# Shifted-window block on one core: another order for the first tile and the tail, 32-column tiles for two small products

## The reference, cut to what matters

```python
xn = _ln2d(x, norm1_g, norm1_b)
xn = jnp.roll(xn, shift=(-SHIFT, -SHIFT), axis=(2, 3))
windows = _window_partition(xn, win)
attn_out = _mha(windows, in_w, in_b, out_w, out_b)   # softmax(q k^T / sqrt(8)) v, 8 heads
attn_out = attn_out @ proj_w.T + proj_b
y = shortcut + roll_back(window_reverse(attn_out))
z = _ln2d(y, norm2_g, norm2_b)
z = einsum('bchw,oc->bohw', z, fc1_w) + fc1_b
z = gelu(z)
z = einsum('bchw,oc->bohw', z, fc2_w) + fc2_b
return y + z
```

## Time and profile before

| | |
|---|---|
| median of 3 runs | 104.44 us (103.73 to 104.53) |
| the profiled execution | 104.1 us, of which 102.3 us are the span from first to last instruction |
| mean granted TensorE clock | 0.977 of full speed |
| busy: PE, PEld | 88.7 us (87%), 55.4 us |
| busy: DVE, ACT, POOL | 64.0, 46.9, 39.6 us |
| the chain that ended last | PE 51%, DVE 12%, POOL 12%, issue 11%, ACT 7%, DMA 4% |

### The profile page before, as it was taken

The page is one execution under the profiler, slowest core; times in us unless marked ns, Lnnn a source line. Parts: engine busy times, 40 slices in busy tenths (PEclk is TensorE's granted clock), DMA queues, the critical chain, the costliest instruction groups (busy, mean ns, idle before and its releaser), DMA issues.

```text
span 102.3 us, 4188 instructions
## 1 busy us (share of the span) xinstructions
PE 88.7 (87%) x1786; PEld 55.4 (54%) x1786; DVE 64.0 (63%) x168; ACT 46.9 (46%) x77; POOL 39.6 (39%) x52
## 2 busy tenths in 40 slices
PE   5999986539999989999999999989899699998550
PEld 5888862224666657668657656667566433323100
DVE  5466699768576978966976979799255713120120
ACT  0511935240954647539537442345434773834400
POOL 7069891796970742940340613407030303000000
PEclk9999999995999999999999999999999999999997
DMA  2898010111111110111110110000000000211202
GB/s 46 211 435 343 13 44 26 51 51 48 39 51 45 39 57 26 44 39 35 57 39 31 39 45 22 3 6 3 6 0 6 0 0 6 103 43 59 103 0 103
DMA packets 3523, 5.93 MB, mean 58 GB/s; under 512 B 1136, under 2 KB 1520, under 8 KB 3376
## 3 DMA queue, kind: packets, MB, share of 16 engines
q1 hardware_dynamic: 2784, 3.28, 9.4%
q10 hardware_dynamic: 720, 2.38, 6.3%
HBM read 2.64 MB, written 1.05 MB: 36 GB/s over the span
## 4 chain that ended last, share of the span: by engine, by line
PE 51%; DVE 12%; POOL 12%; issue 11%; ACT 7%; DMA 4%; DVEq 0%; POOLq 0%
PE ps_s L266 10%; PE ps_t L318 8%; PE ps_t L399 7%; PE ps_u L335 5%; POOL rstd L797 4%; PE ps_m L388 4%; ACT probs L711 4%; DMA x_tok<-x_tok_d 4%; PE ps_t L266 3%; PE ps_o L349 3%; PE ps_m L375 2%; POOL xhat L804 2%; DVE row_max L526 2%; ACT hidden L739 2%; DVE sums L540 2%
## 5 line engine op out<-in xcount | busy, mean ns | idle before, releaser
L711 ACT ACTIVATE probs<-ps_t 128x1024 f32<-128x1024 f32 x16 | 16.4, 1025 | 22.1 <-PE ps_t L318 22.1
L526 DVE TENSOR_REDUCE row_max<-ps_s 128x16 f32<-128x1024 f32 x16 | 19.4, 1215 | 6.1 <-PE ps_s L266 6.1
L266 PE MATMUL ps_s<-masked,qk 32*64 32x256 f32 x256 | 18.4, 402 | 1.6 <-ACT probs L711 0.9
L821 POOL TENSOR_TENSOR rstd<-y_var,minus_half 128x4 f32<-128x4 f32 x8 | 8.1, 1008 | 27.9 <-DVE y_var L569 27.8
L266 PE MATMUL ps_t<-masked,qk 32*64 32x256 f32 x256 | 18.4, 403 | 0.3 <-ACT probs L711 0.3
L318 PE MATMUL ps_t<-max_x,minus_sel 128*128 128x512 f32 x32 | 12.2, 463 | 0.2 <-POOL max_x L812 0.2
L266 PEld LDWEIGHTS ps_s<-masked,qk 32*64 32x64 f32 x256 | 8.8, 136 | 4.7 <-issue 2.8
L335 PE MATMUL ps_u<-probs,vz 128*32 128x64 f32 x512 | 10.5, 222 | 0.0
L812 POOL TENSOR_TENSOR max_x<-max_t,early 128x512 fp32r<-128x512 f32 x8 | 8.4, 1051 | 3.8 <-DVE max_t L534 3.8
L335 PEld LDWEIGHTS ps_u<-probs,vz 128*32 128x32 f32 x512 | 7.9, 109 | 3.6 <-issue 3.2
L232 PE MATMUL ps_t<-zeros 128*128 128x128 f32 x52 | 8.9, 329 | 1.0 <-DVE zeros L639 1.0
(11 more groups left out here) (80 smaller groups left out, 134.8 us busy)
## 6 DMA issues: line engine op xcount, KB each, us to landing
masked<-qk SPq DMA_DIRECT2D x60, 32.0 KB, 1.8
x_ch<-x_ch_d ACTq DMA_DIRECT2D x1, 1024.0 KB, 8.1
out_d<-result SPq DMA_DIRECT2D x4, 256.0 KB, 2.5
x_tok<-x_tok_d ACTq DMA_DIRECT2D x1, 512.0 KB, 6.1
late<-late_d ACTq DMA_DIRECT2D x1, 352.0 KB, 5.3
x_tok<-x_tok_d SPq DMA_DIRECT2D x2, 128.0 KB, 4.2
x_tok<-x_tok_d ACTq DMA_DIRECT2D x1, 256.0 KB, 4.9
early<-early_d ACTq DMA_DIRECT2D x1, 182.0 KB, 4.2
```

What stands on the lines that cost most here:

```text
L266: return nc.tensor.matmul(ps[L * u:L * u + L, g, n * TOK:(n + 1) * TOK], qk[r:r + RG, b, w, t], masked[r:r + RG, b, :, w, t], start=(n == ...
L526: nc.vector.tensor_reduce(row_max[:, 16 * w:16 * w + 16], ps_s[:].rearrange("q g (h j) -> q (g h) j", j=L), axis=AX.X, op=ALU.max).then_in ...
L711: nc.scalar.activation(probs[:, w, :], ps_t[:].rearrange("q g c -> q (g c)"), ACT.Exp).then_inc(probs_done, 1)
L821: nc.gpsimd.tensor_tensor(rstd2[:].rearrange("q n w -> q (n w)"), y_var[:].rearrange("q n w -> q (n w)"), minus_half[:], op=ALU.pow).then_ ...
```

## The change

- **First tile.** The identity matrix is loaded by a DMA of its own. `project_qkv(0)` is split: `project_qk(0)` first, `project_v(0)` after the scores of the tile. ScalarE copies q and k image by image, and the masks for k are made image by image (VectorE three of four heads, ScalarE one). Tile 1's transpose and projection use `ps_u` and `ps_o` (`proj_bank`), the scores of tile 0's image 1 use `ps_t` (`score_bank`). `late_products` and `late_weights` move behind them. A `first_slot` replaces slot 0 on PE, ScalarE has its own order for it. Fewer products of zeros are made.
- **Zeroing.** Four of the five `vz` buffers are zeroed by ScalarE (before its first copy) instead of GpSimd, the masked buffer 3 by VectorE at the start, buffer 2 by GpSimd at the start.
- **Tiles of the array.** `project_out` and `y_spread` use four column tiles of 32 where they used two of 64: 8 matmuls each instead of 4.
- **Tail.** `fc1(0, 0)` moves into slot 7; `fc1(0, 1)` and `fc1(1, 0)` stand ahead of `y_spread(6)` and `project_out(7)`; `y_sum(7)` moves behind `fc2(0)` and `fc1(1, 1)`; `fc2(1)` ahead of `y_spread(7)`.

```diff
         early = sb("early", [P, EARLY])
+        ident_sb = sb("ident_sb", [P, P])
+        ident = ident_sb[:]
         late = sb("late", [P, LATE])
-        ident = early[:, 0:P]
...
+        ps_uo = bank("ps_uo", 2)
+        ps_u, ps_o = ps_uo[:, 0:1, :], ps_uo[:, 1:2, :]
...
+        def proj_bank(k):
+            return ps_uo if k == 1 else ps_m
+
+        def score_bank(k, w):
+            return ps_t if k == 0 and w == 1 else ps_s
...
-            def project_qkv(k):
+            def project_qk(k):
                 pe.wait_ge(xn_copied, k + 1)
...
-                        nc.tensor.matmul(ps_m[C * s:C * s + C, w, 0:TOK], w_qkv[r, C * s:C * s + C], xn[r, k % 2, :],
-                                         start=True, stop=True, tile_position=(C * w, C * s))
+                        ins = nc.tensor.matmul(proj_bank(k)[C * s:C * s + C, w, 0:TOK], w_qkv[r, C * s:C * s + C],
+                                               xn[r, k % 2, :], start=True, stop=True, tile_position=(C * w, C * s))
+                ins.then_inc(qk_projected, 1)
+
+            def project_v(k):
+                if k == 0:
+                    pe.wait_ge(qk_copied, 1)
                 for n in range(BLK):
...
+                ins.then_inc(v_projected, 1)
+
+            def project_qkv(k):
+                project_qk(k)
+                project_v(k)
...
-                if w == 0 and k == 0:
-                    pe.wait_ge(k_masked_first, 2)
+                if k == 0:
+                    pe.wait_ge(k_masked_dve, w + 1)
+                    pe.wait_ge(k_masked_act, w + 1)
...
-                if k + w >= 1:
+                if k >= 1:
                     pe.wait_ge(max_found, 2 * k + w)
...
+                if k + w == 0:
+                    pe.wait_ge(max_found, 2)
...
+                    pe.wait_ge(w_fc1_made, 1)
...
                 for u in range(2):
-                    for w in range(2):
-                        ins = nc.tensor.matmul(o4[C * w:C * w + C, :, u, :], w_out[:, u, :], attn[:, w * P:(w + 1) * P],
-                                               start=True, stop=True, tile_position=(0, C * w))
+                    for j in range(4):
+                        w, c = j // 2, 32 * (j % 2)
+                        ins = nc.tensor.matmul(o4[32 * j:32 * j + 32, :, u, :], w_out[:, u, c:c + 32],
+                                               attn[:, w * P:(w + 1) * P], start=True, stop=True, tile_position=(0, 32 * j))
...
-                    for w in range(2):
-                        ins = nc.tensor.matmul(spread_bank(k)[C * w:C * w + C, n * P:(n + 1) * P],
-                                               rstd2[:, n, w:w + 1].to_broadcast([P, C]), ident,
-                                               start=True, stop=True, tile_position=(0, C * w))
+                    for j in range(4):
+                        ins = nc.tensor.matmul(spread_bank(k)[32 * j:32 * j + 32, n * P:(n + 1) * P],
+                                               rstd2[:, n, j // 2:j // 2 + 1].to_broadcast([P, 32]), ident,
+                                               start=True, stop=True, tile_position=(0, 32 * j))
...
-                pe.wait_ge(z_done, 2 * s + 2)
+                pe.wait_ge(z_done, TILES - 2 if s == 0 and m == 1 else 2 * s + 2)
...
                 pe.wait_ge(late_loaded, 16)
+                pe.wait_ge(v_copied, 2)
...
+            def first_slot():
+                scores_t(0, 0)
+                x_transpose(2)
+                shift_scores(0, 0)
+                late_products()
+                project_qkv(2)
+                scores_both(1, 0, 0, 1)
+                shift_scores(0, 1)
+                x_transpose(3)
+                weigh_values(0, 0)
+                scores(1, 1)
+                fc1_mean()
+                bias_of_v()
+                project_qkv(3)
+                x_transpose(4)
...
                 else:
+                    fc1(0, 0)
                     scores_t(t, 1)
...
-                if t == 0:
-                    fc1_mean()
-                    bias_of_v()
...
-            warm_up(4)
...
+            warm_up(4)
             x_transpose(0)
-            warm_up(2)
+            warm_up(1)
...
-            project_qkv(0)
-            pe.wait_ge(b_qk_made, 1)
-            late_products()
+            project_qk(0)
             warm_up(4)
             x_transpose(1)
-            warm_up(2)
+            scores(0, 0)
             project_qkv(1)
-            scores(0, 0)
-            x_transpose(2)
             scores(0, 1)
-            project_qkv(2)
-            x_transpose(3)
-            for t in range(TILES):
+            project_v(0)
+            first_slot()
+            for t in range(1, TILES):
                 slot(t)
             weigh_values(TILES - 1, 1)
             y_sum(TILES - 2)
-            fc1(0, 0)
+            fc1(0, 1)
...
+            fc1(1, 0)
             y_spread(TILES - 2)
...
             project_out(TILES - 1)
-            fc1(0, 1)
-            fc1(1, 0)
-            y_sum(TILES - 1)
             fc2(0)
             fc1(1, 1)
+            y_sum(TILES - 1)
             fc1(2, 0)
+            fc2(1)
             y_spread(TILES - 1)
-            fc2(1)
             fc1(2, 1)
             fc1(3, 0)
...
+            def mask_k_first(w):
+                if w == 0:
+                    dve.wait_ge(qk_first_copied, 1)
+                else:
+                    dve.wait_ge(qk_copied, 1)
+                for h in range(3):
+                    ins = nc.vector.tensor_scalar(masked[0:C, 0, h, w], qk[C:P, 0, w], slot_mask[C:P, h:h + 1], None,
+                                                  op0=ALU.mult)
+                ins.then_inc(k_masked_dve, 1)
...
-                dve.wait_ge(vz_zeroed, VB)
+                dve.wait_ge(vz_zeroed, 1)
+                dve.wait_ge(vz_zeroed_act, VB - 1)
...
+            for b in (0, 3):
+                nc.vector.memset(masked[:, b].rearrange("q h w t -> q (h w t)"), 0.0).then_inc(masked_zeroed[b], 1)
...
-            mask_k_first()
-            late_weights()
+            mask_k_first(0)
+            mask_k_first(1)
             find_max(0, 0)
             ln1_stats(3)
             find_max(0, 1)
             transpose_max(0)
-            nc.vector.memset(masked[:, 3].rearrange("q h w t -> q (h w t)"), 0.0).then_inc(masked_zeroed[3], 1)
+            late_weights()
...
+            def copy_qk_first():
+                act.wait_ge(qk_projected, 1)
+                act.wait_ge(b_qk_made, 1)
+                for w in range(2):
+                    nc.scalar.activation(qk[:, 0, w], ps_m[:, w, 0:TOK], ACT.Identity,
+                                         bias=b_qk[:, 0:1]).then_inc(qk_copied if w else qk_first_copied, 1)
+
             def copy_v(k):
+                if k == 0:
+                    act.wait_ge(v_projected, 2)
                 if k < VB:
-                    act.wait_ge(vz_zeroed, k + 1)
+                    act.wait_ge(vz_zeroed, 1)
+                    act.wait_ge(vz_zeroed_act, VB - 1)
...
-                for h in range(2, SLOTS):
-                    ins = nc.scalar.activation(masked[0:C, 0, h], qk[C:P, 0], ACT.Copy, scale=slot_mask[C:P, h:h + 1])
-                ins.then_inc(k_masked_first, 1)
+                for w in range(2):
+                    nc.scalar.activation(masked[0:C, 0, 3, w], qk[C:P, 0, w], ACT.Copy,
+                                         scale=slot_mask[C:P, 3:4]).then_inc(k_masked_act, 1)
...
             act.dma_start(early[:], early_d).then_inc(early_loaded, 16)
+            act.dma_start(ident_sb[:], ident_d).then_inc(ident_loaded, 16)
...
+            act.wait_ge(zeros_set, 1)
+            for b in range(1, VB):
+                nc.scalar.activation(vz[:, b].rearrange("q w n h e -> q (w n h e)"), zeros[:, 0:1].to_broadcast([P, 1024]),
+                                     ACT.Copy).then_inc(vz_zeroed_act, 1)
             copy_xn(0)
-            copy_qk(0)
+            copy_qk_first()
             mask_k_first()
-            copy_v(0)
             copy_xn(1)
             copy_qk(1)
             copy_v(1)
+            copy_v(0)
             copy_xn(2)
+            exponentiate(0, 0)
             copy_qk(2)
             copy_v(2)
+            exponentiate(0, 1)
             copy_xn(3)
-            for t in range(TILES):
+            copy_qk(3)
+            copy_v(3)
+            copy_xn(4)
+            for t in range(1, TILES):
...
             nc.gpsimd.memset(minus_half[:], -0.5).then_inc(half_set, 1)
             zero_masked(1)
+            zero_masked(2)
+            zero_values(0)
             pool.wait_ge(half_set, 1)
-            ln1_rstd(0)
-            ln1_scale(0)
-            zero_values(0)
-            ln1_rstd(1)
-            ln1_scale(1)
-            ln1_rstd(2)
-            ln1_scale(2)
-            zero_values(1)
-            zero_masked(2)
-            ln1_rstd(3)
-            ln1_scale(3)
+            for k in range(4):
+                ln1_rstd(k)
+                ln1_scale(k)
```

(2 more changed lines are left out.)

82 lines of the change are left out of this document (42 added, 40 removed).

## The result

The changed kernel took 112.96 us in the median (111.64 to 113.87) beside 104.34 us before: 1.0756 times as long, with a 95% interval of 1.07 to 1.0813. The forecast was 107.7 us, with a range that ended at 109.6. The sign was right and the size was not: the kernel is slower by over twice the forecast amount.

The account below looks back on a forecast made before the run. It took the first tile as bound by circular waits among engines, slots 3 and 4 by a PE-VectorE-GpSimd loop, the tail by project_out(7). Terms -0.5, -0.3 and +4.3 made +3.5, giving 107.7 us, range 105.6 to 109.6.

Parts of the forecast that it names:

- the lowered clock: Tail: rival that the new holes lower TensorE's granted clock, adding 1.4 us for 109.1 us; chance 12%.
- Opening, zeroings at 1.05 each: Opening: four ScalarE zeroings of 1.05 us ahead of the first xn copy put it at 9.7, about 0.85 us late.
- VectorE's second zeroing: Opening: VectorE's second zeroing, 1.76 us, ends near 5.0, making the moments 0.3 us late, covered by ScalarE.
- Early scores, first shift: First tile: scores at 12.4 against 14.95, tile 0's max_x at 17.9, first shift at 19.0, over 5 us early.
- Slot 1 starts at 29.9: End of the first tile: slot 1 at 29.9 against 30.40, a gain of 0.5 us.
- the first tile wins more: First tile: rival with ScalarE's zeroings near their low bound and VectorE on time at 22.9; 1.0 to 2.5 us more, chance 18%.
- shorter than the one that did it: Tail: new holes of 1.5, 2.1 and 1.5 us are shorter than the 2.88 us hole that lowered the clock.
- 32-column tiles, -0.3: project_out and y_spread: 0.11 us saved per slot on a mode switch, counted in slots 2, 5 and 6; gain 0.3 us.
- Slot 7, +0.8 and 0.3 given back: Slot 7: fc1(0, 0), about 1.0 us, goes into a 0.26 us hole; loss 0.8 us, of which 0.5 is left.
- Tail order, +4.3 with slot 7: Tail: project_out(7), gelu(0, 1) and fc2(0) come later, last result at 102.9 against 98.60; +4.3 us, slot 7's 0.5 included.
- faster after all: First tile: rival that all PE idle time and lowered clock there go, slot 1 before about 25; 102.5 us, chance 5%.

Follow-up runs that it names:

- e14: Changed kernel with PE's old tail order and the old, larger counts of zero products in the opening: 105.95 us, ratio 1.018.
- e15: Changed kernel with PE's old tail order and 5 + 1 products of zeros in the first tile's two holes: 104.31 us, ratio 1.0003.
- e5: Changed kernel with PE's old tail order, the opening's old zero-product counts and 5 + 1 products of zeros in the first tile's holes: 104.21 us, ratio 0.9931.
- e10: Kernel before with the new tail and products of zeros in its holes, but fc1(1, 0) back behind project_out(7): 107.09 us, ratio 1.0292.
- e12: e7 with another tail order on PE, ScalarE and VectorE, two gelus moved ahead on ScalarE: 100.35 us, ratio 0.9642 to the kernel before.
- e18: e12 with project_out and y_spread on two column tiles of 64 again: 100.56 us, ratio 0.9658.
- e11: Kernel before with only fc1(0, 0) moved into slot 7: 106.38 us, ratio 1.0113.
- e3: Changed kernel with 6, 8 and 4 products of zeros in the tail's three holes: 111.18 us, ratio 1.061.
- e9: Kernel before with the new tail and products of zeros in two holes, but y_sum(7) back ahead of fc2(0): 106.79 us, ratio 1.026.
- e7: e5 with the projection of tile 3 moved ahead of scores(1, 1): 102.25 us, ratio 0.9809 to the kernel before.
- e1: Changed kernel with PE's tail order as before and fc1(0, 0) out of slot 7: 106.87 us beside 104.02.
- e2: Kernel before with the new tail order and fc1(0, 0) in slot 7 alone: 109.75 us, ratio 1.0548.
- e13: Changed kernel, new tail included, with all products of zeros of e3, e4 and e5: 108.39 us, ratio 1.04.
- e16: e5 with project_out and y_spread on two column tiles of 64 again: 104.15 us, ratio 0.9936.
- e4: Changed kernel with 5 + 1 products of zeros in the first tile's two holes: 110.51 us, ratio 1.0611.

## Why the prediction was right and wrong, step by step

The step that failed is the walk of PE's new order at 2.4 GHz durations, with the lowered clock put aside as a rival of 12% in the tail alone. The runs show half clock in two stretches in its place, worth 2.43 us in the first tile and 1.65 in the tail.

- **Opening, zeroings at 1.05 each: nearly.** They took 0.97 (3.88 for four), `xn` came at 9.18 instead of 9.7. PE's transpose, for which the copy also waits, ends at 8.94, so the zeroings hold `xn` up by 0.24 and not by the 0.85 that I charged.
- **VectorE's second zeroing: small miss.** The second of the two starts 0.38 us after the first ends, and the moments began at 5.32, not 5.0. ScalarE's zeroings covered it, as said.
- **Early scores, first shift: right and a bit early.** 11.92 against 12.4, `max_x` 17.37 against 17.9, shift 18.47 against 19.0. The hole of 1.56 us ahead of tile 4's transpose is the forecast 1.5.
- **"Slot 1 starts at 29.9": the step that failed first.** I walked the new order with durations at 2.4 GHz and asked about the clock only for the tail. The clock fell at 19.7 and cost 2.43 us by slot 1 (e14 against e15). Without it slot 1 starts at 29.05, 0.85 before the forecast. That leans to the rival "the first tile wins more". Its reason holds in part: 0.53 of the 0.85 were there at the first shift, and VectorE began its maximum of tile 1 at 23.15 in e5, against 23.9 in the forecast and 22.9 in the rival; `w_fc_s` took 0.34, as the forecast's 0.4 had it. So the gain was undersized and then lost.
- **The lowered clock as a rival of 12%, in the tail alone: the main error.** The step was "shorter than the one that did it": I took the 2.88 us hole of the earlier trace rows for a measure of what is needed, when it is one case. It fell after 1.35 and 0.41, after 1.56 (sometimes), after 1.64 and after 2.06 us, and in e10 after nothing longer than 0.54. In the tail it cost 1.65, against the 1.4 that the rival gave. The rival was well priced, in one of its two places, and far too unlikely.
- **32-column tiles, -0.3: wrong.** The 0.11 a switch is there (0.47 in place of 0.58). But of the three slots in which I counted it, little is left (0.1 in all, e12 against e18), and holes without a releaser in after's middle slots cost more. I had no term for them.
- **Slot 7, +0.8 and 0.3 given back: right in size, the return was not seen.** +0.74 in after, +0.73 in e11. In e11 `y_msq` comes 3.54 us behind the second shift, as before (3.53).
- **Tail order, +4.3 with slot 7: right.** e3 gives 3.57 + 0.73. Both mechanisms hold by themselves: `project_out(7)` behind `fc1(1, 0)` and then gelu(0, 1) behind `square_y(7)` (e10, 1.73 us), ScalarE's `square_mean(7)` ahead of gelu(1, 0) (e9, 1.60 us). Gelu(0, 1) started 1.53 us after `project_out(7)`, against 1.77. In all the waits behind slot 7 cost 3.57, against 3.5.
- **The range.** Its upper end, 109.6, had room for one low stretch and not for two, nor for the holes in the middle.
- **Two slips of arithmetic, neither of weight.** The median lies 0.3 above the profiled execution, so 107.6 gives 107.9 and not 107.7. In the rival "faster after all", 3.8 us of idle time and 1.2 of lowered clock make 5.0 and not 5.6, so 103.1.

What the account of the profiled execution leaves: of +7.52 us, 4.30 are the tail's waits and slot 7, about 4.1 are two stretches at half clock (2.43 and 1.65), 0.5 is the middle, and 1.35 was won in the first tile (4.30 + 4.08 + 0.48 - 1.35 = 7.51). The middle's part has no experiment of its own: it is smaller than the 0.8 us by which the hole of slot 3 lengthens that slot, and what makes that hole is not known. The median lies 1.3 us above this execution; the others ran at 0.90 to 0.94 instead of 0.947, and where they lost it no trace shows.

## What to carry over

When an order is changed on an engine whose clock is gated, list the holes that the new order opens anywhere, with their lengths, and give each a price at the half clock for the work behind it; one observed hole that did lower the clock says nothing about shorter ones, and one trace in which it held says little about the next execution. Price a move on one engine by what is queued behind it on the others: here two products on PE cost 3.3 us through two activations that stood in the wrong order on ScalarE, and another order with ScalarE's list changed too won 1.2. When time is to be bought from waits, look first for real work to put into the hole (e7), and fill it with products of zeros only where there is none.

## What the runs showed of the hardware

- The granted clock went to 0.50 after holes of 1.35 and 0.41 us with 1.5 us of work between (after, e14), after 1.07 (e1), after 1.64 (e11), after 2.06 (after; 2.04 in e2) and, in e13 and e15 but not in e5 and e16, after 1.56 us. In e10 it fell after holes of 0.51, 0.54 and 0.40, which the kernel before has too without falling there; and it held after 1.75 in after, though not after the same 1.75 in e4. So the length of the last hole does not tell by itself. With rows identical to 0.01 us from 7 us up to that point, whether it falls differs by execution (e5, e13).
- Five and one products of zeros in the first tile brought slot 1 forward by 2.4 us, and 18 in the tail made the tail 1.65 us shorter.
- PE stood still within a group of scores with no releaser, for 0.39 us at 50.22 in after and for 0.40 at the same place in e14. Slot 3's shifts are 4.20 us apart in after, 4.42 in e14 and 4.17 in e5, and 3.39 in e15 and e16; in slot 2 they are 3.99 apart in e10 and 3.66 in the kernel before, where others have 3.39. What it is stays open; it was not tested.
- The same `w_fc_s` multiply of 128x256 elements took 3.32 us in the earlier trace rows and 0.34 in after, with GpSimd's zeroings gone from beside it. The Trainium skill (SBUF — State Buffer, section on the two separate sides) has GpSimd and VectorE in a two-port mode exclude each other on a shared port pair; the two figures agree, though no run here changed that alone.
- An activation that only writes 128x1024 zeros takes 0.97 us, nearly as long as a gelu of the same size (1.11).
